# Loading the A adapters in sixteen 256-byte-run transfers so that W is transposed at 16-byte steps

## The reference, cut to what matters

```python
x = x + ffn(cond(x, cond_A, cond_B, itok), base_w, base_b, ffn_A, ffn_B, router_w)   # x: 8 x 512 x 2048

def cond(x, A, B, ids):                 # per batch: one of 8 adapters, rank 16
    Bx  = einsum('bni,bri->bnr', x, B[ids])
    return einsum('bnr,bor->bno', Bx, A[ids])            # A: 8 x 2048 x 16

def ffn(x, base_w, base_b, A, B, router_w):
    base_out   = einsum('bsi,oi->bso', x, base_w) + base_b     # base_w ("W"): 2048 x 2048
    res_hidden = einsum('bsi,ri->bsr', x, A)                   # 64 x 2048
    logits     = einsum('bsi,ei->bse', x, router_w)            # 16 experts, top 2 of the softmax
    delta      = einsum('bse,bsr,eor->bso', combine, res_hidden, B)   # B: 16 x 2048 x 64
    return base_out + delta * 0.5
```

## Time and profile before

| | |
|---|---|
| median of 3 runs | 462.93 us (459.8 to 463.29) |
| profiled execution | 459.67 us |
| its span, first to last instruction | 457.4 us (2.3 us less) |
| mean granted TensorE clock | 0.991 |
| busy share of the span | PE 90%, DVE 68%, ACT 24%, POOL 9% |
| moved by DMA | 135.30 MB, mean 296 GB/s |

### The profile page before, as it was taken

The page is one execution under the profiler, slowest core; times in us unless marked ns, Lnnn a source line. Parts: engine busy times, 40 slices in busy tenths (PEclk is TensorE's granted clock), DMA queues, the critical chain, the costliest instruction groups (busy, mean ns, idle before and its releaser), DMA issues.

```text
span 457.4 us, 6130 instructions
## 1 busy us (share of the span) xinstructions
PE 413.4 (90%) x2240; PEld 275.5 (60%) x2240; DVE 312.7 (68%) x702; ACT 107.5 (24%) x163; POOL 40.5 (9%) x53
## 2 busy tenths in 40 slices
PE   0687996799888999999999999999999999999996
PEld 0466884576555675566567556655675566566675
DVE  3699699698457557766767675677667766757353
ACT  0002033345563240132013102400230132123210
POOL 3020000002100120012001101200120012002000
PEclk9998999899999999999999999999999999999999
DMA  8999999899999998898989998988998899555835
GB/s 230 362 335 334 336 377 346 267 234 322 333 320 235 346 348 267 282 347 301 296 287 367 306 289 294 367 269 292 331 334 282 289 361 309 194 195 196 322 148 185
DMA packets 90383, 135.30 MB, mean 296 GB/s; under 512 B 5506, under 2 KB 43442, under 8 KB 90354
## 3 DMA queue, kind: packets, MB, share of 16 engines
q1 hardware_dynamic: 63680, 102.08, 67.2%
q10 hardware_dynamic: 26674, 32.84, 23.9%
HBM read 99.23 MB, written 35.65 MB: 295 GB/s over the span
## 4 chain that ended last, share of the span: by engine, by line
PE 68%; DVE 13%; DMA 12%; issue 2%; ACT 2%; ACTq 2%; DVEq 0%
PE ps L871 13%; PE ps L892 12%; PE ps L893 10%; PE ps L894 10%; DMA early_u<-in_L_ffn_B 7%; PE ps L905 7%; PE ps L895 5%; DMA xbuf<-in_L_ffn_base_w 5%; PE ps L826 3%; DVE xT L706 3%; DVE h_r L687 3%; PE ps L836 3%; DVE early L639 3%; ACT bexpT L473 2%; DVE xbuf L814 2%
## 5 line engine op out<-in xcount | busy, mean ns | idle before, releaser
L814 DVE TENSOR_TENSOR xbuf<-ps,xbuf 128x512 f32<-128x512 f32 x128 | 86.9, 679 | 110.4 <-PE ps L895 110.2
L892 PE MATMUL ps<-h_r,u_r 128*128 128x512 f32 x256 | 109.4, 427 | 7.1 <-DVE xbuf L814 7.1
L893 PE MATMUL ps<-h_r,u_r 128*128 128x512 f32 x256 | 100.3, 392 | 0.0
L894 PE MATMUL ps<-h_r,u_r 128*128 128x512 f32 x256 | 100.1, 391 | 0.0
L836 PE MATMUL ps<-early 128*128 128x256 f32 x256 | 65.7, 409 | 20.3 <-DVE early L639 20.2
L892 PEld LDWEIGHTS ps<-h_r,u_r 128*128 128x128 f32 x256 | 48.0, 188 | 47.6 <-issue 20.1
L706 DVE STREAM_TRANSPOSE xT<-xbuf 128x512 f32<-128x512 f32 x112 | 72.0, 681 | 0.0
L836 PEld LDWEIGHTS ps<-early 128*128 128x128 f32 x256 | 49.5, 204 | 32.9 <-issue 17.6
L639 DVE STREAM_TRANSPOSE early<-xbuf 128x256 f32<-128x256 f32 x128 | 66.1, 581 | 4.3 <-issue 3.7
L871 PE MATMUL ps<-bexpT,cur 128*32 128x512 f32 x512 | 61.6, 598 | 2.2 <-DVE h_r L687 1.5
L473 ACT ACTIVATE h_r<-ps 128x512 fp32r<-128x512 f32 x64 | 35.7, 594 | 87.6 <-issue 54.9
(11 more groups left out here) (67 smaller groups left out, 207.1 us busy)
## 6 DMA issues: line engine op xcount, KB each, us to landing
out<-xbuf SPq DMA_DIRECT2D x31, 1024.0 KB, 7.0
xbuf<-in_x SPq DMA_DIRECT2D x28, 1024.0 KB, 7.0
xbuf<-in_x SPq DMA_DIRECT2D x32, 512.0 KB, 8.4
xbuf<-in_x ACTq DMA_DIRECT2D x32, 512.0 KB, 9.5
xbuf<-in_L_ffn_base_w SPq DMA_DIRECT2D x16, 512.0 KB, 18.6
xbuf<-in_L_ffn_base_w ACTq DMA_DIRECT2D x16, 512.0 KB, 19.1
gm_r<-g_hilo SPq DMA_DIRECT2D x128, 32.0 KB, 6.5
early_u<-in_L_ffn_B SPq DMA_DIRECT2D x12, 256.0 KB, 15.5
```

The source lines that it names most:

```text
L814: dve.tensor_tensor(xs, ps[:, ACC + t % 2, :], xs, ALU.add).then_inc(s_out, 1)
L892: pe.matmul(acc, u_r[:, b.q, 0, h, tok_t], hi, start=(h == 0), stop=False)
L893: pe.matmul(acc, u_r[:, b.q, 0, h, tok_t], lo, start=False, stop=False)
L894: pe.matmul(acc, u_r[:, b.q, 1, h, tok_t], hi, start=False, stop=False)
```

## The change

A is laid out with four neighbouring features to a partition. Each group of 32 partitions covers its 512 features in four blocks j of 128: partition i of the group holds the features 128j + 4i to 128j + 4i + 3. Four features of rank 16 are 256 bytes in DRAM, where 16 were 1024 bytes. A transfer handles one group and one block, so there are sixteen transfers of 64 KB (eight on each queue) for two of 512 KB. A step of W then takes the features 128j + 4l + r, that is steps of 4 elements, 16 bytes. The transposes of ffn_A and router_w become four of 384 elements for two of 768. `take_a`, the products and all else stay; line numbers behind `load_cond_a` move by up to 4.

```diff
+    AR = 4
+    AJ = KD // AR
-    condA_q = cond_A.rearrange("n (p r) k -> p n (r k)", p=P)
+    condA_q = cond_A.rearrange("n (q j i r) k -> q i n j (r k)", q=NQ, j=AJ, i=SQ)
...
         def load_cond_a(eng, h):
-            half = slice(h * (P // 2), (h + 1) * (P // 2))
-            eng.dma_start(conda_q[half], condA_q[half]).then_inc(s_conda, 16)
+            for q in (2 * h, 2 * h + 1):
+                to_j = conda_q[q * SQ:(q + 1) * SQ].rearrange("p n (j f) -> p n j f", j=AJ)
+                for j in range(AJ):
+                    eng.dma_start(to_j[:, :, j], condA_q[q, :, :, j]).then_inc(s_conda, 16)
...
             def take_a():
-                dve.wait_ge(s_conda, 32)
+                dve.wait_ge(s_conda, 16 * NQ * AJ)
...
             def ffna_transposes():
-                by_r = ffna_q.rearrange("p t (l r) -> p r t l", l=SQ)
+                by_r = ffna_q.rearrange("p t (j l r) -> p j r t l", l=SQ, r=AR)
                 to_r = ffnaT.rearrange("p r (t l) -> p r t l", l=SQ)
-                for h in range(2):
-                    part = slice(h * KD // 2, (h + 1) * KD // 2)
-                    dve.transpose(to_r[:, part], by_r[:, part]).then_inc(s_fat, 1)
+                for j in range(AJ):
+                    dve.transpose(to_r[:, j * AR:(j + 1) * AR], by_r[:, j]).then_inc(s_fat, 1)
...
             def w_transpose(n):
-                src = w_in[g % WB].rearrange("p t (l r) -> p r t l", l=SQ)[:, s]
+                src = w_in[g % WB].rearrange("p t (j l r) -> p j r t l", l=SQ, r=AR)[:, s // AR, s % AR]
```

More of the change, by code:

```diff
@@ L493, in copy_experts @@
                 act.wait_ge(s_ef, g + 1)
-                for at, there, count in ((0, s_a, NB), (0, s_bT, KC), (1, s_fat, 2), (1, s_sm, 1),
+                for at, there, count in ((0, s_a, NB), (0, s_bT, KC), (1, s_fat, AJ), (1, s_sm, 1),
                                          (2, s_xe, KD)):
@@ L847, in ga_products @@
             def ga_products():
-                pe.wait_ge(s_fat, 2)
+                pe.wait_ge(s_fat, AJ)
                 for s in range(KD):
```

## The result

| | median | lowest to highest | runs |
|---|---|---|---|
| before | 461.08 us | 459.08 to 464.42 | 20 |
| changed | 464.53 us | 463.35 to 466.49 | 20 |

The ratio is 1.0073 with a 95% interval of 1.0055 to 1.0092. The changed kernel is 3.4 us slower, 0.7%. Its profiled execution took 465.47 us, with a span of 463.6 us. So the two profiles differ by 5.8 us where the medians differ by 3.4, and what stands in them has to be weighed with this in mind. (In spans it is 6.2 us, 463.6 less 457.4.)

The account below looks back on a forecast made before the run. The DMA backlog ending in E6's load was taken to bound the W stage, PE the batches. A's load +3.9 us and transposes -0.6 us gave +3.3 us, 466.2 us (+0.7%), with a range of 459.5 to 474 us.

Parts of the forecast that it names:

- What A costs: Start of the kernel, DMA engines: loading A in 256-byte packets adds +3.9 us, from bounds of +1.2 to +11.3.
- part 3: Queue issues of A at the start: eight per queue instead of one take 4.2 us, or 5.8 us at 0.73 each.
- part 4: DMA cost of A's 4096 packets: four prices, 15, 20, 28 or 59 ns each; 28 ns (7.2 us) underlies the forecast.
- the lowest bound: Cheapest price for A's 256-byte packets: only bytes count, 15 ns, A stays at 3.8 us; issues stretch it by 1.2 us.
- The estimate of 7.6 us: Loading A, if packets below 512 bytes mean each byte moved twice: 7.6 us instead of 3.8, +3.8.
- the higher bound of 581: W's transposes on DVE: 581 ns at 16-byte steps, nothing gained over 64-byte steps; the lower bound was 419 ns.
- two readings of the note on cachelines: W's transposes: first, each access crossing to a new 16-byte line pays (581 ns); second, striding is free to 4 fp32 (419).
- The term of -0.6 us: Behind F6 in the W stage: faster transposes remove 0.25 us of waiting and 0.37 us of product lag, 0.6 us gained.
- Packets at 59 ns: Rival on A's load: small packets cost nearly as much as large; at 59 ns +10.7 us, 473.6 us; chance 0.28.
- A faster stream from gentler reads: Rival on the DMA stream from 15 to 88 us: it gains 3.4 us, net -2.8 us, 460.1 us; chance 0.08.
- DVE as the bound: Rival in the W stage: DVE's transposes set the time after all, net -6.2 us, 456.7 us; chance 0.08.
- The fourth rival: Step buys nothing or A's layout doesn't matter: transposes 581 ns, A's packets at the bytes' price, +1.2 us, 464.1; chance 0.06.

## Why the prediction was right, point by point

- **The bound: right.** The DMA backlog, which ends in E6, sets F6; DVE, 10 of 10 us busy, does not. Transposes 166 ns faster brought F6 no earlier (89.5 us), and the delay at the start passed to F0, F5 and F6 as 3.2, 3.1 and 3.3 us.
- **What A costs: +3.9 forecast, +3.3 in the profile, 2.1 and 2.2 in two others; the size was near, the reason wrong in the main.** The issues (part 3) were right: eight in 3.85 us for 4.2, W0's first at 4.63 us for 5.0. The price of a packet (part 4) was not. I had taken 28 ns, 7.2 us for A. In the trace 1014 packets of 256 bytes pass in the microsecond from 5 to 6 us, that is 16 ns each and 4.0 us for all 4096, almost what the lowest bound (bytes alone, 15 ns) says; of part 4's four prices the first was the true one. The estimate of 7.6 us, with each byte moved twice, is not borne out either. The loss comes just behind A. ACT's queue begins W only at about 10 us, so SP's works nearly alone on 64 partitions, 218 GB/s from 8 to 10 us, and the stream then runs at 272 for 364 GB/s up to 15 us. This step stood nowhere in my sum, beyond 0.5 us for idle engines. Shown for its first part: the low rate whenever SP's queue is alone on the lower partitions, also with A in two transfers, and F6 13.1 us late when both queues write to one side. Its second part, the larger in bytes, has no cause shown. How the delay divides between the number of transfers and the length of runs is not settled.
- **The transposes: wrong in sign.** I took 419 ns from 64-byte and unstepped rows; it was 602, above the higher bound of 581, for which I had seen no reason. A step of 16 bytes costs no less than one of 64, but 21 ns more for each transpose. Of the two readings of the note on cachelines in the Trainium skill ("SBUF — State Buffer", Door 1: The DMA port swizzle) the measurement decides for the first: every access that crosses to a new line pays. The term of -0.6 us became about +1 us by the waits behind F6 (0.92 + 0.29 - 0.25); as a time it is 0.14% (-0.17% to 0.45%), not clear of nothing. The 419 ns themselves hold for a read without a step: 415.
- **The sum.** 3.3 us were forecast, 3.4 measured (1.0073, with an interval of 2.5 to 4.2 us). In absolute terms it is 466.2 against 464.53 us, since the median of before, over 20 runs, was 461.08 and not 462.93. That the two differences agree so closely is luck. A's delay was taken 0.6 us too large by the changed kernel's profile, 1.8 by another, and for a wrong reason; the transposes were taken 1.6 us too small; the two errors offset each other.
- **The rivals.** Packets at 59 ns: excluded, 1014 a microsecond. A faster stream from gentler reads: the reads became no gentler, and without steps at all F6 didn't move. DVE as the bound: excluded by the same run. The fourth rival had both of its premises right, packets at the price of their bytes and no gain from the step, and comes to +1.2 us, below the interval of 2.5 to 4.2: it lacks the same step as my sum. That its 464.1 lies next to the measured 464.53 is due to the lower median of before.
- **What I had said would show it.** A's last landing about 4 us after 9.7: 11.8, only 2.1 later, which goes against the price of a packet. First transpose at 19 us: 18.46. F6 at 92.5: 92.14. First tile at 122.6: 125.53, where the lower clock behind F6 (1.7 us) and slower transposes added 2.9. PE's waits at F4 to F6 did not grow (none, 2.82 and 2.56 us for 0.58, 3.56 and 2.41): that hung on the 419 ns.

## What to carry to other kernels

An engine that is busy for 10 of 10 us may still have next to nothing to give: look for the column that never falls below 1, here the DMA share, and for the wait at which it drains. When a load at the head of a saturated stream is cut up, ask not only what its packets cost but whether both queues still reach the next large load together, and on which partitions they write meanwhile. A stall with ready work behind it, like PE's at F5 and F6, is the cheaper thing to mend: moving three flips and two loads in the tables gave 0.4%, while transposes without any step, more than the layout had hoped for, gave 0.3% at best guess and not clear of nothing. And where one profile is compared with one other, first ask how far two profiles of the same stream lie apart, here about 1 us.

## What the runs showed of the hardware that was not expected

- Both queues on the same 64 partitions: 284 and 287 GB/s in two windows of 10 us, for 340 and 348 on opposite halves (in two others 338 and 361 for 348 and 374), and 4.3% in the kernel's time.
- One queue alone: 204 to 218 GB/s into the lower 64 partitions, 408 over all 128.
- Reads of fp32 by the transpose: 415 ns for 256 elements without a step, 579 to 592 at 64 bytes, 602 to 610 at 16 bytes.
- Packets of 256 bytes pass at 1014 a microsecond (244 GB/s), 12% below the 276 GB/s of 1 KB packets in the first microseconds of the kernel before.
- In five profiles the granted clock fell to 0.50 just behind F6 and stayed there for some 3 us: in the changed kernel, both with cut-up A in the old layout, the one without steps and the one with W's groups dealt out otherwise. PE had waited 2.56 to 4.19 us there. It did not fall in the one with the ids behind A, where PE had waited 2.87 us. Behind F6 a fall costs 0.9 to 1.7 us (4.05 to 4.87 us for seven products, 3.19 without it). It fell elsewhere too, in the kernel before at about 43 and 80 us, where the next wait for a load takes the loss up, so that F6 is no later. What decides it is open.
